# Two of a head pair's 32 row-maximum units copied by ScalarE and reduced on GpSimd, with twelve value segments per pair

## The reference

```python
xn = _layernorm(x, axis=-1)
# attention: 16 heads of 16, with the linear bias of ALiBi
scores = jnp.einsum('bqhd,bkhd->bhqk', Q, K) * scale
scores = scores + _alibi_bias(S, H, x.dtype)[None]
attn = jax.nn.softmax(scores, axis=-1)
out = jnp.einsum('bhqk,bkhd->bqhd', attn, V).reshape(B, S, D)
# experts: top 2 of 8, hidden 352, and a shared one of hidden 704
h = jax.nn.silu(jnp.einsum('tc,ech->eth', xf, W1)) * jnp.einsum('tc,ech->eth', xf, W2)
y = jnp.einsum('eth,ehc,te->tc', h, W3, w)
y = y + (silu(xf @ Ws1) * (xf @ Ws2)) @ Ws3
x = x + attention(xn) + experts(xn)
```

## Time and profile before

| what | value |
|---|---|
| median of 3 runs | 2384.82 us |
| span of the profiled execution, first to last instruction | 2353.9 us |
| the median less that span | 30.9 us |
| TensorE busy / VectorE / ScalarE / GpSimd, whole span | 98% / 84% / 73% / 43% |
| pairs 2 to 17, between transposes at 244.2 and 557.9 us | 313.7 us |
| pairs 18 to 25, to 709.3 us | 151.4 us |
| pairs 26 to 57, to 1317.0 us | 607.7 us |

### The profile page before, as it was taken

How to read it: one execution, slowest core, us unless ns; L and a number is a source line. 1 busy time by engine, 2 the same in 40 slices (tenths; PEclk the granted TensorE clock), 3 DMA queues, 4 the chain that set the end, 5 groups by cost and what they waited for, 6 DMA issues and landing times.

```text
span 2353.9 us, 50539 instructions
## 1 busy us (share of the span) xinstructions
PE 2316.8 (98%) x19358; PEld 1543.2 (66%) x19358; DVE 1978.7 (84%) x2874; ACT 1709.7 (73%) x3276; POOL 1012.1 (43%) x1013
## 2 busy tenths in 40 slices
PE   7999999999999999999999999999999999999998
PEld 6875444444444444444444438999999989888998
DVE  7888999999999999999999966777777765555555
ACT  4447888888999999998999997777777753333332
POOL 2112556553225555454454334434343354455444
PEclk9999999999999999999999999999999999999999
DMA  8994544543224444343343335777777753344432
GB/s 295 375 338 173 169 155 161 165 145 99 81 83 131 125 123 136 114 128 118 121 127 109 108 96 192 241 240 236 242 236 247 233 174 108 108 129 125 123 108 90
DMA packets 189745, 383.07 MB, mean 163 GB/s; under 512 B 54164, under 2 KB 100756, under 8 KB 176292
## 3 DMA queue, kind: packets, MB, share of 16 engines
q1 hardware_dynamic: 151536, 219.17, 29.1%
q0 software_dynamic: 36880, 159.87, 21.3%
q10 hardware_dynamic: 1088, 0.79, 0.1%
HBM read 247.86 MB, written 140.31 MB: 165 GB/s over the span
## 4 chain that ended last, share of the span: by engine, by line
PE 65%; DVE 29%; issue 3%; ACT 2%; DMA 1%; SPq 0%; POOL 0%; DVEq 0%; POOLq 0%; ACTq 0%
PE ps L569 62%; DVE mx L1054 17%; DVE mx L1051 10%; PE ps L582 3%; DMA Md<-mT 1%; ACT ptb L889 0%; ACT pta L889 0%; ACT qkH L869 0%; DMA xr<-Xn 0%; DMA OPS<-Md 0%; DVE mT L1070 0%; SPq L1562 0%; DMA xt<-in_x 0%; DVE qkL L1041 0%; POOL rstd L1270 0%
## 5 line engine op out<-in xcount | busy, mean ns | idle before, releaser
L569 PE MATMUL ps<-OPS 54*128 54x512 f32 (+1 forms) x4096 | 734.7, 439 | 5.2 <-DMA OPS<-Md 2.4
L1054 DVE TENSOR_REDUCE mx<-ps 128x2 f32<-128x1024 f32 x620 | 734.2, 1216 | 5.7 <-PE ps L569 4.8
L569 PEld LDWEIGHTS ps<-OPS 54*128 54x128 f32 (+1 forms) x4096 | 366.3, 184 | 394.0 <-ACT pta L889 263.7
L889 ACT ACTIVATE pta<-ps 128x512 f32<-128x512 f32 x1024 | 549.7, 605 | 65.5 <-PE ps L569 56.8
L889 ACT ACTIVATE ptb<-ps 128x512 f32<-128x512 f32 x1024 | 544.9, 609 | 47.4 <-PE ps L569 38.8
L1051 DVE TENSOR_REDUCE mx<-ps 128x1 f32<-128x512 f32 x808 | 514.0, 677 | 2.1 <-PE ps L569 2.0
L569 PE MATMUL ps<-OPS,WB 128*128 128x256 f32 (+2 forms) x2364 | 384.5, 315 | 3.1 <-DVE VB L1181 1.5
L569 PEld LDWEIGHTS ps<-OPS,WB 128*128 128x128 f32 (+1 forms) x2364 | 332.3, 183 | 28.2 <-issue 3.9
L569 PE MATMUL ps<-pta,VB 128*32 128x192 f32 (+7 forms) x4520 | 324.7, 370 | 0.0
L569 PE MATMUL ps<-ptb,VB 128*32 128x512 f32 (+1 forms) x3064 | 296.9, 461 | 0.0
L1314 POOL TENSOR_SCALAR m<-m 128x16 f32<-128x16 f32 x64 | 16.9, 265 | 540.8 <-DVE m L1064 540.8
(11 more groups left out here) (172 smaller groups left out, 2867.5 us busy)
## 6 DMA issues: line engine op xcount, KB each, us to landing
OPS<-QKh SPq DMA_DIRECT2D x512, 64.0 KB
Xs<-zero POOLq DMA_DIRECT2D x71, 256.0 KB, 3.6
xr<-Xs SPq DMA_DIRECT2D x71, 256.0 KB, 5.3
Ys<-VB SPq DMA_DIRECT2D x71, 256.0 KB, 5.0
QKh<-qkH SPq DMA_DIRECT2D x16, 1024.0 KB, 7.3
QKl<-qkL SPq DMA_DIRECT2D x16, 1024.0 KB, 8.8
OPS<-QKl SPq DMA_DIRECT2D x256, 64.0 KB
asum<-Sd SPq DMA_DIRECT2D x64, 256.0 KB
```

Source lines behind the costliest of these rows:

```text
L569: return self.e.matmul(o, l, r, start=start, stop=stop)
L889: self.e.activation(pt(m)[:, half * GT:(half + 1) * GT], ps[:, score_bank(n), :], ACT.Exp).then_inc(sem["exp"], 1)
L1054: self.e.reduce_max(mx[:, r % 2, hh, i, :], ps[:, bank - 1:bank + 1, :], AX.X).then_inc(sem["mxred"], 2)
```

## The change

Units 0 and 8 of each pair from pair 2 on (COPIED) are no longer reduced by VectorE. ScalarE copies each from PSUM to a buffer `mst` in SBUF (`max_unit` of Scalar). At the place of unit 8, GpSimd takes both copies from 512 to 64 columns in three levels; a level is max(a - b, 0) + b on the two halves, so three steps, each of which waits for the one before (`copied_max`; semaphore mxl). VectorE reduces the 64 columns that are left (`finish`, after unit 1 of the next pair). DOUBLE falls to five couples, so 20 singles. The fold moves from unit 0 to unit 3 of the next pair (FOLD_AT), and with it the negation on GpSimd, which stood at unit 31. Each string of PAIR has three value segments at new places, twelve in a pair with new widths, where there were thirteen. Whoever waited for a unit's reduction waits for the copy where the unit is copied (`taken`, `maxima_over`).

```diff
@@ -46,19 +46,22 @@
 MAX_BANKS = (2, 3, 7)
 FIRST_PAIR = "SuSuSuLSuSuLSuSuLSu", "SuSuSuPSuSuSuPSuSuTP", "SuSuSuPSuSuSuPSuSuP", "SuSuSuPSuSuSuPSuSuP"
 PAIR = (
-    "SuSuPSuSuPSuSuSuPSu",
-    "SuSuPSuSuPSuSuSuPSuT",
-    "SuSuPSuSuSuPSuSuSuP",
-    "SuSuPSuSuPSuSuPSuSuP",
+    "SuPSuSuSuPSuSuPSuSu",
+    "SuPSuSuSuPSuSuPSuSuT",
+    "SuPSuSuSuPSuSuPSuSu",
+    "SuPSuSuSuPSuSuPSuSu",
 )
 TAIL = "SSSSSSSSP"
 TAIL_AT = 8 * (NPAIR - 2) + 2
 TAIL_BANKS = (0, 1, 2, 4, 5, 6, 7)
 FIRST_WIDTHS = 352, 320, 352
-WIDTHS = 224, 288, 512, 288, 320, 512, 416, 512, 352, 160, 128, 192, 192
+WIDTHS = 416, 256, 352, 512, 256, 256, 416, 320, 288, 448, 288, 288
 TAIL_WIDTHS = WIDTHS[0:3] + 3 * (2 * 512,), 4 * (2 * 512,), FIRST_WIDTHS
 STREAM = 8 * 512
-DOUBLE = (0, 2, 5, 7, 8, 9, 10, 11, 12, 14)
+DOUBLE = (1, 5, 9, 13, 15)
+COPIED = (0, 8)
+NC = len(COPIED)
+FOLD_AT = 3
 KMAX, KEXP = 52, 54
 NPT = 8
 SCAT_AT = 26
...
@@ -87,6 +90,20 @@
 def score_bank(n):
     tail = n - 4 * TAIL_AT
     return n % 3 if tail < 0 else TAIL_BANKS[tail % 7]
+
+
+def copied(n):
+
+    return n >= 64 and n % 32 in COPIED
+
+
+def copies(n):
+
+    return 0 if n < 64 else (n - 64) // 32 * len(COPIED) + sum(u < n % 32 for u in COPIED)
+
+
+def reduced(n):
+    return n - copies(n)
 
 
 class Turn:
@@ -507,6 +524,8 @@
         B.close()
 
 
+        mst = WB0[:, 2 * P:2 * P + 2 * NC * GT].bitcast(F32).rearrange("p (k s n) -> p k s n", k=2, s=NC)
+
         C = ExitStack()
         OH, OL = (sbuf(C, n, [P, 2, GT], F32R) for n in ("OH", "OL"))
         sbuf(C, "sparec", [P, 2048])
@@ -554,6 +573,17 @@
             for k in range(3):
                 w.wait_ge(f"xn{k}", 16 * len(range(k, NG, 3)))
 
+        def taken(w, n):
+
+            if copied(n):
+                w.wait_ge("mxcp", copies(n + 1))
+            else:
+                w.wait_ge("mxred", reduced(n + 1))
+
+        def maxima_over(w):
+            w.wait_ge("mxred", reduced(32 * NPAIR))
+            w.wait_ge("mxcp", copies(32 * NPAIR))
+
         def attention_over(w):
             for k in range(2):
                 w.wait_ge(f"ox{k}", 16 * NPAIR // 2)
@@ -636,7 +666,7 @@
                 if at >= 4:
                     was, j = ring.turns[at - 4]
                     if was == "max":
-                        self.w.wait_ge("mxred", j + 1)
+                        taken(self.w, j)
                     else:
                         self.w.wait_ge("rtc", j + 1)
                 else:
...
@@ -906,6 +936,15 @@
                         self.e.copy(counts[:, :, :].rearrange("p n e -> p (n e)"), ps[:, ring.bank("count", j), :]
                                     ).then_inc(sem["rtc"], 1)
 
+            def max_unit(self, n, bank=None):
+                if not copied(n):
+                    return
+                r, u = divmod(n, 32)
+                self.w.wait_ge("vmm", 4 * NG)
+                self.w.wait_ge("mxf", r - 3)
+                self.w.wait_ge("mxmm", n + 1)
+                self.e.copy(mst[:, r % 2, COPIED.index(u), :], ps[:, ring.bank("max", n), :]).then_inc(sem["mxcp"], 1)
+
             def split_block(self, b, i):
                 if b > NBLK + 2 or b == 0:
                     return
@@ -1046,20 +1085,36 @@
                 u = n % 32
                 r, hh, i, half = unit(n)
                 bank = ring.bank("max", n) if bank is None else bank
-                if u // 2 not in DOUBLE or r < 2:
+                if copied(n):
+                    pass
+                elif u // 2 not in DOUBLE or r < 2:
                     self.w.wait_ge("mxmm", n + 1)
                     self.e.reduce_max(mx[:, r % 2, hh, i, half:half + 1], ps[:, bank, :], AX.X).then_inc(sem["mxred"], 1)
                 elif half:
                     self.w.wait_ge("mxmm", n + 1)
                     self.e.reduce_max(mx[:, r % 2, hh, i, :], ps[:, bank - 1:bank + 1, :], AX.X).then_inc(sem["mxred"], 2)
-                if u == 0 and r:
+                if u == 1 and r:
+                    self.finish(r - 1)
+                elif u == FOLD_AT and r:
                     self.fold(r - 1)
                 elif n == 32 * NPAIR - 1:
+                    self.finish(r)
                     self.fold(r)
 
+            def finish(self, r):
+
+                if r < 2:
+                    return
+                hh, i, side = unit(32 * r + COPIED[0])[1:]
+                last = unit(32 * r + COPIED[-1])[2]
+                self.w.wait_ge("mxl", 9 * (r - 1))
+                self.e.tensor_reduce(mx[:, r % 2, hh, i:last + 1:(last - i) // (NC - 1), side], mst[:, r % 2, :, 0:64],
+                                     AX.X, ALU.max).then_inc(sem["mxf"], 1)
+
             def fold(self, r):
 
-                self.w.wait_ge("mxred", 32 * (r + 1))
+                self.w.wait_ge("mxred", reduced(32 * (r + 1)))
+                self.w.wait_ge("mxf", r - 1)
                 self.w.wait_ge("mnl", r - 1)
                 self.e.tensor_reduce(m16[:, r % 2, :, :], mx[:, r % 2, :, :, :], AX.X, ALU.max).then_inc(sem["m16"], 1)
 
@@ -1306,18 +1361,44 @@
                 e.memset(zero[:, :], 0.0).then_inc(sem["zmem"], 1)
 
             def max_unit(self, n, bank=None):
+                r, u = divmod(n, 32)
+                if copied(n):
+                    self.copied_max(n)
+                if u == FOLD_AT and r:
+                    self.negate(r - 1)
+                elif n == 32 * NPAIR - 1:
+                    self.negate(r)
+
+            def copied_max(self, n):
+
                 e = self.e
                 r, u = divmod(n, 32)
-                k2 = r % 2
-                if u == 31:
-                    self.w.wait_ge("m16", r + 1)
-                    e.tensor_scalar(m16[:, k2, :, :], m16[:, k2, :, :], -1.0, None, ALU.mult).then_inc(sem["mng"], 1)
-                    self.w.wait_ge("mtr", r - 1)
-                    self.w.wait_ge("mng", r + 1)
-                    e.tensor_copy(mneg[:, k2, :, 0, :].bitcast(F32R), m16[:, k2, :, :]).then_inc(sem["mnh"], 1)
-                    self.w.wait_ge("mnh", r + 1)
-                    e.tensor_tensor(mneg[:, k2, :, 1, :], m16[:, k2, :, :], mneg[:, k2, :, 0, :], ALU.subtract
-                                    ).then_inc(sem["mnl"], 1)
+                if u != COPIED[-1]:
+                    return
+                m = mst[:, r % 2, :, :]
+                self.w.wait_ge("mxcp", copies(n) + 1)
+                done = 9 * (r - 2)
+                for level in range(3):
+                    half = 256 >> level
+                    a, b = m[:, :, 0:half], m[:, :, half:2 * half]
+                    self.w.wait_ge("mxl", done + 3 * level)
+                    e.tensor_tensor(a, a, b, ALU.subtract).then_inc(sem["mxl"], 1)
+                    self.w.wait_ge("mxl", done + 3 * level + 1)
+                    e.tensor_scalar(a, a, 0.0, None, ALU.max).then_inc(sem["mxl"], 1)
+                    self.w.wait_ge("mxl", done + 3 * level + 2)
+                    e.tensor_tensor(a, a, b, ALU.add).then_inc(sem["mxl"], 1)
+
+            def negate(self, r):
+
+                e, k2 = self.e, r % 2
+                self.w.wait_ge("m16", r + 1)
+                e.tensor_scalar(m16[:, k2, :, :], m16[:, k2, :, :], -1.0, None, ALU.mult).then_inc(sem["mng"], 1)
+                self.w.wait_ge("mtr", r - 1)
+                self.w.wait_ge("mng", r + 1)
+                e.tensor_copy(mneg[:, k2, :, 0, :].bitcast(F32R), m16[:, k2, :, :]).then_inc(sem["mnh"], 1)
+                self.w.wait_ge("mnh", r + 1)
+                e.tensor_tensor(mneg[:, k2, :, 1, :], m16[:, k2, :, :], mneg[:, k2, :, 0, :], ALU.subtract
+                                ).then_inc(sem["mnl"], 1)
 
             def heads(self, r, i):
                 if i == 1:
```

More of the change, by code:

```diff
@@ L71 @@
     "xt qkmm vmm mxmm smm pv obmm rtmm sct gmm up down sdn "
-    "wsplh woh xh qkh vev exp acc1 rte rtc wsh sch sg hh yev och "
-    "wspll bq wol ob st ag ve norm xl qkl mxred m16 mtr rcp rt rtw wslv scl hf hl ocl s1 gf fin "
-    "nhalf rstd lgc pad vcp ones zmem mng mnh mnl nrm rg rtd rtm rtp rtb rts wslp xb ya"
+    "mxcp wsplh woh xh qkh vev exp acc1 rte rtc wsh sch sg hh yev och "
+    "mxf wspll bq wol ob st ag ve norm xl qkl mxred m16 mtr rcp rt rtw wslv scl hf hl ocl s1 gf fin "
+    "mxl nhalf rstd lgc pad vcp ones zmem mng mnh mnl nrm rg rtd rtm rtp rtb rts wslp xb ya"
 ).split()
@@ L673, in scores @@
                 elif tail < 7:
-                    self.w.wait_ge("mxred", 32 * NPAIR)
+                    maxima_over(self.w)
                 else:
```

## The result

The changed kernel takes 2700.61 us (median of 4 runs, 2696.55 to 2704.60) against 2383.89 of the kernel before on the same chip: ratio 1.1334, 95% interval 1.1318 to 1.1350. Its profiled execution took 2701.29 with a span of 2699.5. The forecast was 2544, and 2650 its high end. The direction and the mechanism came out as forecast; the forecast's +159 us is half of the 317 us that the change cost.

What follows compares the result with a forecast made beforehand. VectorE bounded the kernel, TensorE 0.3 us a pair behind; after the change GpSimd's loop would. Pairs 2-17 +56, 18-25 +4, 26-57 +98, last three +1: +159 on 2384.8 gives 2544 us, range 2440 to 2650.

Steps and rivals of the forecast that it cites:

- The loop: GpSimd's chain per pair, raise, Sd, asum, scaling, negation, nine steps, sets the pace: 19.3 us, 21.9 with scatters; chance 0.86.
- The waits listed as its signs: Scaling waits for asum in nearly every pair, VectorE's transpose for GpSimd's negation; the negation's 7.4 us fold wait is gone.
- nine steps, and the hand-over to them: GpSimd's dependent steps per pair: 4.97 us two-input, 1.46 one-input, 0.8 hand-overs, sum 7.2; low bound 5.8.
- The asum load: SP's broadcast load of the sums, from issue to GpSimd's scaling: 5.1 us, from rows of 4.80 and 6.25.
- The one-input step: GpSimd's one-input part of each level: 0.65, 0.46 and 0.36 us, at the copy's slope of 0.78 ns an element.
- as dear as two inputs: Upper bound for GpSimd's nine steps, with one-input steps at the two-input price: 8.4 us a pair.
- Dearer than summed: Rival: one-input steps at two-input price (+1.1) and asum at 6.25 (+1.15) in 59 pairs: 2674 us; chance about 0.05.
- This difference should stay: The timed median, 2384.8, stands 30.9 us above the profiled span of 2353.9, and was expected to remain so.
- TensorE's clock: Half speed for 3.4 us after TensorE's wait costs 1.7 us a pair, 19.9, lying under 21.9: no term.
- VectorE's gain of 0.65 a pair: VectorE's reductions fall from 18.5 to 17.65 us a pair, less some 0.2 for the last maximum over 2 x 64.
- the faster rival: GpSimd's loop stays hidden under TensorE's 18.2; pairs take 18.2 to 18.7 us, kernel 2355 us; chance 0.05.
- equal rivals: At about 4 us for GpSimd's nine steps, quiet pairs' gains cancel the others' losses: 2385 us; chance 0.02.

Runs made afterwards that it cites:

- no_steps: The changed kernel without the nine GpSimd steps; VectorE reduces both copies itself over all 2 x 512 columns: 2412.09 us.
- one_late: steps_late with one level of three on GpSimd (three steps), VectorE reducing 2 x 256 columns: 2370.10 us, 0.9935 of the kernel before.
- steps_late: The changed kernel with the nine GpSimd steps issued eight units later, behind the raise to -1 and one scatter: 2379.49 us, 0.9982 of the kernel before.
- loads_behind: The changed kernel with SP's store of the scaled sums put ahead of the next pair's loads, so nothing directly follows asum: 2602.07 us.
- two_late: steps_late with two levels of three on GpSimd (six steps), VectorE reducing 2 x 128 columns: 2356.01 us, 0.9888 of the kernel before.
- mult_late: The changed kernel with GpSimd's scaling moved from after the next pair's first string to after its third, ahead of the raise: 2474.41 us, 1.0378 of the kernel before.

## Why the prediction was right in direction and short in size

**The loop: right.** The waits listed as its signs came. Scaling waited for asum in 19 of 20 pairs from 800 to 1300 us, the transpose waited for the negation in all 20, the negation's wait for the fold was gone, and the clock fell below 1.00. The first of these is no proof: scaling waited for asum 24 times in `no_steps` and in `one_late` too, where the loop did not set the pace; the transpose's wait is in neither over these 500 us. The signs with a size did not come: scatter pairs take 25.3 us and not 21 to 23, quiet ones 22.3 and not 19.3, and VectorE is at 73% in the scatter stretch and not at 80 to 90. `steps_late` undoes only the place of the steps and gets 321 us back.

**Its length: short by 3.2 us in the mean scatter pair and 2.8 in the mean quiet one.** One turn, that of 1029.99 to 1055.44, took 25.45 us, against the sum of 21.9:

| term | forecast | measured |
|---|---|---|
| raise, and its hand-over to SP | 2.96 + 0.1 | 3.02 |
| Sd to asum | 1.7 | 1.43 |
| asum to scaling | 5.1 | 7.26 |
| scaling and two scatters | 3.58 | 3.53 |
| negation to the next start | 0.86 | 1.15 |
| row load | 0.3 (mean) | 0.61 |
| nine steps, and the hand-over to them | 7.2 + 0.1 | 8.45 |

Two terms were sized too small. *The asum load*, 5.1, "nearer the quiet one, since the four-partition-group broadcast is the same transfer each time": the quiet row, 4.80 at 1395.46, stands where SP's list has run out of operand loads (nothing else is issued there up to 1404); the 6.25 row had them 2.6 us behind. A late loop holds SP at Sd, so all that is queued goes out right behind asum, and the load takes 7.1. Neither row had that state, and the upper bound of 6.25 was no bound. `loads_behind` shows the cause. *The one-input step*, whose slope was taken from the copy, 0.78 ns an element: it has 2.55, (1503 - 524)/384, and is dearer than a two-input step. The bound "as dear as two inputs" is 1.5 x 4.97 + 0.8 = 8.3 by its own terms, not 8.4; 8.45 came, since the three one-input steps took 2.87 in place of 2.48 and the hand-overs 0.6 in place of 0.8. The load is 2.16 too small and the nine steps 1.15, together 3.3 of the 3.55 us by which this turn was short; negation and row load are 0.3 too small each, and the way from Sd to asum 0.3 too large. The rival "Dearer than summed" had both, with the load too small still (its time is 2544 + 133 = 2677, not 2674).

**"This difference should stay" (30.9): wrong.** The changed kernel's time stands 1.8 above its span. The step put 29 us onto the forecast and so hid part of the shortfall: without it the forecast would have been 2515, and the pieces show the whole shortfall: 2699.5 - 2512.7 = 187 us, of which 103 in pairs 26 to 57, 38 in pairs 2 to 17, 23 in the quiet eight and 23 at the two ends. There the same loop runs in the last three whole pairs (22.7 each), which is about 11; another 12 us come ahead of the transpose at 255.9, of which 7 are left in `steps_late`, without the loop.

**TensorE's clock: it fell, and its cost shows in no term.** The means of 0.88 and 0.89 come from stretches at full and at half speed (2.4 and 1.2 GHz) after TensorE stood waiting, and `two_late` has 1.00 with no such wait. A mean of 0.89 over 25.3 us takes 2.8 us of TensorE's rate a pair, not 1.7. TensorE still stands idle 121 of 809 us in pairs 26 to 57, and the measured terms of the turn hold no step of TensorE, so the clock need not have cost anything; no run holds it apart.

**VectorE's gain of 0.65 a pair: 0.2 at most.** With the loop out of the way quiet pairs take 18.73 (`steps_late`), not 18.2 to 18.7 as the faster rival had it, and each piece of work that VectorE is given shows nearly in full: with 64, 128, 256 and 512 columns `finish` takes 0.28, 0.41, 0.68 and 1.21 us and the quiet pair 18.73, 18.82, 19.10 and 19.63. TensorE may be dearer than its 18.2: in 150 us of `steps_late` it is busy 150 and VectorE 147, and in `two_late` its matmuls have 94% of the chain from 248 to 1313 us. Which one a further saving must come from is open.

**The faster and equal rivals: rightly small** for this order. The faster one's condition was met by moving the steps, not by cheaper ones.

## What to carry to other kernels

Before work is put on a half-idle engine, write down every chain that leaves that engine and comes back within one turn, DMAs included, and add the new work to those it stands in; an idle share says nothing about them. If the chain has a DMA leg in which the engine waits, the work belongs there: moved by a quarter of a pair, the same nine instructions cost 321 us less. Then look again at what the work's new place frees later, as `mult_late` shows. And price a load by a row in which the same transfers stand behind it on its queue, and a row of one profiled execution against a second one before its difference to the median is carried forward.

## What the runs showed of the hardware

- On GpSimd a one-input maximum with a constant took 1503, 845 and 524 ns for 512, 256 and 128 columns, a two-input subtraction 1298, 731 and 458. The Trainium skill's GPSIMD Engine Reference (section 4.1) calls one-input operations there roughly line-rate and puts the penalty on two inputs; here the one-input step is 14 to 16% dearer than the two-input one. The prediction's estimate worked out from the Trainium skill, 4.7 us for the nine steps, is 3.8 us below the measured 8.45.
- A broadcast load of 256 KB on SP's queue landed for its reader 5.0 to 5.4 us after its issue with nothing directly behind it, and 6.9 to 7.1 us with up to nine loads right behind (medians). The mean share of the DMA engines' time hides this: it was 0.33 over the scatter stretch, but 0.95 in the two microseconds from 1038, while the load was under way.
- The same program, unchanged, ran its scatter pairs at 18.9 us in one profiled execution and at up to 20.5 in another, at clock 1.00 in both. What differed between these two was not found.
